# Sort: one predicated copy of the whole payload per compare and exchange step

## What is computed

```python
h = relu(layernorm(x))                       # [50000, 128]
agg = h
for _ in range(3):
    left  = agg[src] @ q_w
    right = tanh(rel * agg[dst] @ k_w)       # rel = edge_emb[edge_type]
    att   = sum(left * right, axis=1)
    w     = softmax of att over the edges with the same src
    agg   = mean over those edges of w * rel * agg[dst], then scaled to norm 1
    out  += agg + h
return x + out
```

## Time and profile before

| | |
|---|---|
| Median of 3 runs | 2115.43 us (2114.66 to 2116.12) |
| Profiled execution, its own time | 2108.43 us |
| Its span, first to last instruction | 2106.6 us |
| VectorE busy | 1358.1 us (64%), 6127 instructions |
| GpSimd busy | 1233.6 us (59%), 1218 instructions |
| TensorE busy (matrix products) | 1085.6 us (52%) |
| ScalarE busy | 842.2 us (40%), 2649 instructions |
| Mean granted TensorE clock | 0.683 of full speed |
| The sort, L768's first start to L775's last end | 11.83 to 181.42 us |

### The profile page before, as it was taken

How to read it: one execution, slowest core, us unless ns; L and a number is a source line. 1 busy time by engine, 2 the same in 40 slices (tenths; PEclk the granted TensorE clock), 3 DMA queues, 4 the chain that set the end, 5 groups by cost and what they waited for, 6 DMA issues and landing times. The chain is left out here.

```text
span 2106.6 us, 23618 instructions
## 1 busy us (share of the span) xinstructions
PE 1085.6 (52%) x5196; PEld 878.5 (42%) x5196; DVE 1358.1 (64%) x6127; ACT 842.2 (40%) x2649; POOL 1233.6 (59%) x1218
## 2 busy tenths in 40 slices
PE   0111354375586585653036769668355874756420
PEld 0001233263374474642024557557233763645410
DVE  8897688667656747885036575775546655579870
ACT  2221567646635544664023244444332422234420
POOL 1002777657757757777777665600474556567776
PEclk9999856556666656655568677785676867665555
DMA  8802555544324323445146455521697779457771
GB/s 234 239 27 95 190 171 195 174 145 141 118 81 118 104 90 112 166 159 177 40 130 211 141 145 138 160 79 72 159 161 176 162 140 192 116 141 209 208 202 35
DMA packets 199662, 302.96 MB, mean 144 GB/s; under 512 B 31696, under 2 KB 113948, under 8 KB 196064
## 3 DMA queue, kind: packets, MB, share of 16 engines
q1 hardware_dynamic: 161120, 228.46, 34.1%
q0 software_dynamic: 38400, 72.99, 17.0%
HBM read 175.89 MB, written 130.86 MB: 146 GB/s over the span
## 5 line engine op out<-in xcount | busy, mean ns | idle before, releaser
L599 POOL DMA_INDIRECT tr<-in_x_dram,tidx x200 | 200.1, 1000 | 315.6 <-DVEq L838 183.9
L599 POOL DMA_INDIRECT tr<-agg_d,tidx x200 | 196.4, 982 | 252.5 <-issue 184.7
L1416 PE MATMUL ps<-rt,wr 128*125 128x128 f32 x1200 | 255.1, 381 | 172.5 <-DVE wr L1003 121.3
L1351 PE MATMUL ps<-ident,rt 128*128 128x128 f32 x600 | 135.0, 367 | 361.2 <-DVE rt L1065 298.7
L1416 PEld LDWEIGHTS ps<-rt,wr 128*125 128x125 f32 x1200 | 223.9, 279 | 188.1 <-DVE wr L1003 132.9
L1198 ACT COPY rtT<-ps 128x512 f32<-128x512 f32 x150 | 88.3, 589 | 514.0 <-PE ps L1351 513.5
L1239 ACT ACTIVATE sqj<-ps,invc 125x128 bf16<-125x128 f32 x600 | 212.5, 373 | 177.4 <-PE ps L1416 177.2
L599 POOL DMA_INDIRECT tr<-ntab_d,tidx x200 | 200.9, 1004 | 104.5 <-issue 61.5
L1351 PEld LDWEIGHTS ps<-ident,rt 128*128 128x128 f32 x600 | 95.0, 189 | 386.0 <-DVE rt L1065 314.8
L611 POOL DMA_INDIRECT out_dram<-rt,lidx x200 | 210.8, 1054 | 69.7 <-issue 60.6
L611 POOL DMA_INDIRECT ntab_d<-rt,lidx x200 | 210.2, 1051 | 60.8 <-issue 60.2
(11 more groups left out here) (229 smaller groups left out, 2264.3 us busy)
## 6 DMA issues: line engine op xcount, KB each, us to landing
agg_d<-rt SPq DMA_DIRECT2D x100, 258.0 KB
xr<-agg_d SPq DMA_DIRECT2D x100, 258.0 KB, 3.9
relr<-rel_d SPq DMA_DIRECT2D x100, 256.0 KB, 5.0
ntab_d<-rt SPq DMA_DIRECT2D x15, 1679.7 KB
rt<-in_x_dram SPq DMA_DIRECT2D x13, 1024.0 KB, 6.5
out_dram<-rt SPq DMA_DIRECT2D x13, 1024.0 KB, 4.1
acc_d<-xr SPq DMA_DIRECT2D x50, 258.0 KB, 3.1
rel_d<-relr SPq DMA_DIRECT2D x50, 256.0 KB, 3.5
```

The source lines that it names most:

```text
L599: G.indirect_dma_start(out=row, out_offset=None, in_=table[:, :], in_offset=bass.IndirectOffsetOnAxis(ap=idx[:, n:n + 1], axis=0)).then_in ...
L1351: ins = T.transpose(ps[B_TR][:, t, :], rt[:, g * GT + t, 0:D], ident[:, :])
L1416: ins = T.matmul(ps[B_T + j % 2][0:R, t, :], wr[:, (j % 2) * GT + t, 0:R], rt[:, j * GT + t, 0:D], start=True, stop=True)
```

## The change

The payload is exchanged by one predicated copy of 256 elements. ScalarE copies the whole payload, 256 elements, into `vold`, which grows from 128 to 256 elements. VectorE then copies, where the mask is set, `vold` with its halves swapped over the whole payload. The mask still has one element per pair; it is read twice, once for each half, by a step of 0, and the halves of `vold` are read in reverse order (`::-1`). `s_vx` now counts one per step, and the table of numbers shrinks to a plain list.

```diff
-        vold = flat[:, 6 * SC:6 * SC + 128]
+        vold = flat[:, 6 * SC:7 * SC]
...
-                va, vb = halves(v)
-                step, n = payload_at[k, m]
+                step = step_of[k, m]
                 gt = bank(2 + step % 2)[:, 0:128].rearrange("p (n s) -> p n s", s=stride)
-                old = vold.rearrange("p (n s) -> p n s", s=stride)
+                new, old = (t.rearrange("p (n t s) -> p n t s", t=2, s=stride) for t in (v, vold))
                 ch.note(V.tensor_tensor(gt, ka, kb, ALU.is_gt))
                 ch.note(V.tensor_tensor(na, ka, kb, ALU.min))
                 ch.note(V.tensor_tensor(nb, ka, kb, ALU.max))
                 dve.wait_ge(s_vc, step + 1)
                 dve.wait_ge(s_dve, ch.at - 2)
-                V.copy_predicated(va, gt.bitcast(I32), vb).then_inc(s_vx, 1)
-                dve.wait_ge(s_vx, n + 1)
-                V.copy_predicated(vb, gt.bitcast(I32), old).then_inc(s_vx, 1)
+                V.copy_predicated(new, gt.bitcast(I32).unsqueeze(2).to_broadcast([P, 128 // stride, 2, stride]),
+                                  old[:, :, ::-1, :]).then_inc(s_vx, 1)
                 ch.join()
...
-                elif n > 0:
-                    act.wait_ge(s_vx, n)
-                stride = 1 << (m - low)
-                A.copy(vold.rearrange("p (n s) -> p n s", s=stride),
-                       v.rearrange("p (n t s) -> p n t s", t=2, s=stride)[:, :, 0, :]).then_inc(s_vc, 1)
+                elif step > 0:
+                    act.wait_ge(s_vx, step)
+                A.copy(vold, v).then_inc(s_vc, 1)
...
-                    pe.wait_ge(s_vx, payload_at[i + 9, i + 8 if way == 0 else 7][1])
+                    pe.wait_ge(s_vx, step_of[i + 9, i + 8 if way == 0 else 7])
```

More of the change, by code:

```diff
@@ L336, in gnn_kernel @@
         s_pace = sem("s_pace")
[L339 to L348, removed]
+        SORT = [(k, m) for k in range(1, LOGN + 1) for m in range(k - 1, -1, -1)]
+        step_of = {km: i for i, km in enumerate(SORT)}
         block = ctx.enter_context(nc.Block())
@@ L811, in _ @@
             assert at == 0
-            dve.wait_ge(s_vx, 2 * len(SORT))
+            dve.wait_ge(s_vx, len(SORT))
             dve.sem_inc(s_go, 1)
@@ L1174, in _ @@
             turns = 0
-            for step, (k, m, n) in enumerate(SORT):
-                v, low = (vT, 8) if m > 7 else (vbuf, 0)
+            for step, (k, m) in enumerate(SORT):
+                v = vT if m > 7 else vbuf
                 if k > 8 and m in (k - 1, 7):
```

## The result

| | before | changed |
|---|---|---|
| Median of 6 runs | 2115.45 us (2112.21 to 2119.7) | 2083.76 us (2077.58 to 2093.83) |
| Ratio | | 0.9858, 95% interval 0.9828 to 0.9887 |
| Profiled execution, its span | 2106.6 us | 2081.2 us |
| The sort's last predicated copy ends at | 181.42 us | 149.55 us |

The median fell by 31.7 us; the interval of the ratio makes that 24 to 36 us. The forecast was 2082.6.

What follows compares the result with a forecast made beforehand. The prediction took VectorE's queue in the sort as the bound. Savings of 19.5 and 14.8 us, less 1.5 at the turns, made 32.8, taken off the median of 2115.43 for 2082.6 us; range 2076 to 2097.

Steps and rivals of the forecast that it cites:

- VectorE's queue bounds the sort, and its end is passed on whole: In the sort, VectorE sets the pace and nothing later has begun, so all 32.8 us saved reach the total.
- One kind of copy at 0.43 to 0.44: In all 120 sort steps the merged copy of 256 elements takes 0.43 to 0.44 us, whatever the stride.
- Slow kind 19.5, fast kind 14.8: The merge saves 19.5 us in 42 steps at strides 1 and 2, and 14.8 in 78 at stride 4 and more.
- ScalarE hides with 0.045: In each sort step ScalarE's longer copy makes a loop of 0.90 us, hidden behind VectorE's 0.945 with 0.045 to spare.
- The turns lose 0.106 each: At 14 places where TensorE transposes keys and payload, ScalarE's longer copy lies bare: 0.106 us each, 1.5 us lost.
- The start of a turn moves with the last predicated copy ... and costs nothing new.: Where TensorE's transposes begin, their start follows the last predicated copy for keys and payload, at no added time.
- the new copy leaves the queue as L775 did: On VectorE the merged copy lets the next instruction start like the old slow copy, costing about 0.135 us above a fast one.
- 1: At strides 1 and 2 the dear copies remain, from short source or mask runs or mask repeats: 12.2 us, 2094.8; chance 0.12.
- 2: Only the 22 stride 1 steps stay dear, through swapped single words: 6.4 us, 2089.0; chance 0.09.
- 4: Repeated mask or swapped source stalls at every stride: slower, 2152, or a draw at 2117.4; chance 0.07.
- 3: ScalarE's copy from SBUF grows to about 0.45 us and its loop becomes the bound: 5 us, 2087.6; chance 0.06.
- 5: Work behind the sort gives some back, as TensorE's clock may fall by elapsed time: 7 us, 2089.6; chance 0.02.

Runs made afterwards that it cites:

- m1_forms: A separate kernel without the computation: VectorE alone runs 18 instruction forms, 16 times each; a predicated copy of 128 elements took 0.302 us in one run, 0.441 at step 2.
- m2_lines: A separate kernel without the computation: 11 further VectorE forms of 128 elements; a predicated copy took 0.722 us at step 4, 0.724 into interleaved halves.
- e4_scalar_late: The changed kernel with one more 128-element ScalarE copy ahead of ScalarE's copy in every step; the sort ended at 168.76 us, one execution took 2082.59.
- e3_merge_long: The kernel before with the merged copy only in the 78 steps of stride 4 and more; 2503.26 us, ratio 0.9969, sort's end 166.96 us.
- the second trace: The changed kernel run again unedited; its span was 2057.3 us, the sort ended at 149.44 and the median was 2070.87.
- e1_two_copies: The changed kernel with two predicated copies of 128 reading ScalarE's full copy, no wait between; 2492.68 us, ratio 0.987 to the kernel before, sort's end 164.35 us.
- e2_merge_short: The kernel before with the merged copy only in the 42 steps of stride 1 and 2; 2506.85 us over four runs, sort's end 163.98 us.

## Why the prediction was right

- *VectorE's queue bounds the sort, and its end is passed on whole.* Held: the sort's end moved by 31.9 us, the median by 31.7 (and by 31.7 again in another set of runs, 2102.57 to 2070.87). That the two agree to 0.2 us, and forecast and median to 1.2, is in part luck: the interval runs from 24 to 36 us.
- *One kind of copy at 0.43 to 0.44.* Held: 0.441, at every stride. The reading that the destination makes the slow kind was an argument from two rows; `m1_forms` and `m2_lines` showed it, and sharpened it: not runs of 4 words, but changes of the aligned 16-byte group.
- *Slow kind 19.5, fast kind 14.8.* Measured, with the turns in them: 17.4 and 14.5. Without turns and phase ends the traces of before and after give 19.7 (20 distances x 0.4725, and 22 x 0.465 for the L773 that goes in the last steps) and 15.6: a fast step gained 0.200 (1.138 to 0.938), not 0.19, as the new copy costs the queue a little less than assumed.
- *ScalarE hides with 0.045.* Held: 0.405 us per copy, loop 0.90, and `e4_scalar_late` shows that it becomes the bound at once beyond that.
- *The turns lose 0.106 each.* Held. The distance from the max to the predicated copy rose from 0.29 to 0.40:

```profile
62.32 0.41 ACT L1174 COPY rt<-rt 128x256 f32<-128x256 f32 x1
62.36 0.28 DVE L761 TENSOR_TENSOR rt<-rt 128x128 f32<-128x128 f32 x1
62.76 0.45 DVE L764 COPY_PREDICATED rt<-ps,rt 128x256 f32<-128x256 int32 x1
```

- *"The start of a turn moves with the last predicated copy ... and costs nothing new."* This step failed, and with it the reading that the new copy leaves the queue as L775 did, where a phase ends. Together they cost 2.0 us; the two kinds of step gave 0.9 more than their terms, and so 32.8 became 31.9. That the sum came out so near is a cancelling of errors. At the inner turns the queue's join waits for the max (L761, before L770), and only behind it is TensorE told to begin. Before, two predicated copies stood between, and the max was long done; now it is waited for bare. The first fence is of the kernel before, the second of the changed one:

```profile
77.56 0.45 DVE L775 COPY_PREDICATED rt<-ps,rt 128x128 f32<-128x128 int32 x1
77.65 0.29 PEld L1293 LDWEIGHTS ps<-ident,rt 128*128 128x128 f32 x2 [3.15 <-DVEq L804]
```

```profile
63.50 0.28 DVE L761 TENSOR_TENSOR rt<-rt 128x128 f32<-128x128 f32 x1
63.70 0.45 DVE L764 COPY_PREDICATED rt<-ps,rt 128x256 f32<-128x256 int32 x1
63.89 0.29 PEld L1281 LDWEIGHTS ps<-ident,rt 128*128 128x128 f32 x2 [2.42 <-DVEq L794]
```

TensorE starts 0.19 behind the last predicated copy, 0.11 behind the max's end, where it was 0.09 behind L775. So it is at six of the seven inner turns. At the seventh (phase 9, with a single step behind the first turn) the copy itself starts 0.39 behind the max, and TensorE 0.09 behind the copy, as before; and in `e3_merge_long`, whose last steps keep two copies, it starts 0.08 to 0.09 behind them at all seven. At the outer turns the cause is another: the sign multiplication stands between, and the max is done before it starts. First before, then changed:

```profile
73.11 0.44 DVE L775 COPY_PREDICATED rt<-ps,rt 128x128 f32<-128x128 int32 x1
73.36 0.32 DVE L787 TENSOR_SCALAR rt<-rt 128x256 f32<-128x256 f32 x1
```

```profile
59.97 0.44 DVE L764 COPY_PREDICATED rt<-ps,rt 128x256 f32<-128x256 int32 x1
60.30 0.35 DVE L777 TENSOR_SCALAR rt<-rt 128x256 f32<-128x256 f32 x1
```

It starts 0.33 behind the predicated copy instead of 0.25, though both copies last 0.44, and lasts 0.03 longer. Within a step the prediction had weighed this rightly, since the slow copy makes the next instruction longer (L768 0.39); at a phase end hardly anything of that comes back. Over the traces the way from the last predicated copy to TensorE's start grew by 0.10 to 0.12 at six inner turns and by 0.11 to 0.13 at the seven outer ones, 1.5 us. The seven phase ends without a turn, which the prediction did not treat, lose 0.07 each in the same way (1.34 to 1.41 from last copy to next first copy), 0.5 us.
- *The rivals.* 1, 2 and 4 are ruled out by the forms (0.444 swapped or not), 3 by ScalarE's 0.405. Against 5 stand the second trace and the granted clock behind the sort: 0.65 before, 0.65 and 0.66 in the two traces of the changed kernel. The rule of the Trainium skill ("Vector Engine (DVE) Microarchitecture Reference", "Measured stream behaviour on trn2") on pairs of adjacent words does not show in any source here: a source at step 2 takes the 0.302 us of one run, swapped single words the 0.444 of the plain copy. Of the Trainium skill's fixed 58 cycles per instruction ("VectorE: DVE Perf Modes", the TRN2 errata) the merge in the fast kind is the test: `e1_two_copies` against the changed kernel, 1.005 to 0.938, is 0.067 us a step, beside the 0.06 estimated from the page. The page's figure fits the merge by itself. The wait is the larger part: 1.138 to 1.005, 0.133 a step.

## What to carry to other kernels

Where an instruction waits for the one ahead of it on the same engine, look first at who made it wait: here an old value was kept for half of the data, and keeping it for all of it removed a wait and an instruction in one. It cost nothing inside the runs of steps, because the other engine had slack, and 1.5 us at the turns, where it had none. Predicated copies should write their destination in order through whole, aligned groups of 16 bytes. And when instructions are taken from in front of a signal, ask what they covered: the join behind them may now be waited for bare (0.1 us at each of six inner turns).

## What the hardware showed that I had not expected

- A predicated write costs 4.4 ns whenever the aligned group of 16 bytes changes, once that is more often than every fourth element (0.302, 0.372, 0.441, 0.72 us for 128 elements with 32, 48, 64, 128 changes; step 8 is a little cheaper, 0.692), with any mask, even of zeros. An ordinary TENSOR_TENSOR pays 0.09 us in 128 elements where every element has a new group, nothing at step 2.
- How much of a copy's duration the queue pays is not told by its duration. Copies of 0.44 us let the next instruction start after 0.23 to 0.25 (128 elements, short destination runs) or 0.33 (256 in one run), but the first kind makes the instruction behind it longer.
- The same kernel can differ far more between sets of runs than the change is worth: the kernel before took 2115.45, 2519.96 and 2102.57 us as a median in three sets. It is not shown that the chip makes the difference: the record gives the set of 2519.96 and a single later execution of 2108.27 the same chip number. The sort does not take part in this: `e2_merge_short` and `e3_merge_long`, traced where the kernel before took 2519.96, ended it within 0.2 us of what the other traces had let expect. Waits for DMAs do, and so do waits of GpSimd for VectorE. In `e1_two_copies`, whose span was 2508.8, GpSimd waited 231.5 us for stores of the running sums, where the kernel before and the changed one had 69.4 and 71.5 in this group; what slowed the stores stays open:

```profile
L591 POOL DMA_INDIRECT tr<-in_x_dram,tidx x200 | 201.5, 1008 | 473.8 <-DMA acc_d<-xr 231.5 <-DVEq L828 167.1 <-issue 74.9
```
